# Layer 1 attention: the causal mask of the row maxima is added by VectorE's max instruction instead of by TensorE matmuls; one copy in layer 0 becomes a max

## The reference, cut to what matters

```
scores = jnp.einsum('bthd,bshd->bhts', q, k) / np.sqrt(HD)
causal = jnp.tril(jnp.ones((seq, seq), dtype=bool))
scores = jnp.where(causal[None, None], scores, -jnp.inf)
attn = jax.nn.softmax(scores, axis=-1)
out = jnp.einsum('bhts,bshd->bthd', attn, v)
```

## Time and profile before

| | us |
|---|---|
| median of 3 runs | 1455.15 |
| lowest, highest | 1451.16, 1457.0 |
| the profiled execution | 1449.74 |
| its span, first to last instruction | 1448.0 |
| PE busy | 1243.9 (86%) |
| DVE busy | 979.8 (68%) |
| ACT busy | 690.4 (48%) |
| POOL busy | 381.1 (26%) |
| mean granted TensorE clock | 0.909 |

### The profile page before, as it was taken

The page is one execution under the profiler, slowest core; times in us unless marked ns, Lnnn a source line. Parts: engine busy times, 40 slices in busy tenths (PEclk is TensorE's granted clock), DMA queues, the critical chain, the costliest instruction groups (busy, mean ns, idle before and its releaser), DMA issues. The chain is left out here.

```text
span 1448.0 us, 20297 instructions
## 1 busy us (share of the span) xinstructions
PE 1243.9 (86%) x7132; PEld 753.8 (52%) x7132; DVE 979.8 (68%) x1750; ACT 690.4 (48%) x1319; POOL 381.1 (26%) x243
## 2 busy tenths in 40 slices
PE   4779999999999999579999967358988888789997
PEld 3444454545455454348888845323433333347886
DVE  4747656565655642579999956757777664448998
ACT  2242544444353434336666644314666657326664
POOL 0036465746656568000000000302111111020000
PEclk9899999999999999689999968657999988869998
DMA  3101202011120200046766500051222201021321
GB/s 109 42 16 36 51 19 66 16 50 34 36 45 16 46 15 31 0 102 138 158 152 142 128 1 1 6 120 37 51 64 63 50 21 39 26 64 44 112 73 30
DMA packets 51471, 81.54 MB, mean 56 GB/s; under 512 B 16748, under 2 KB 34452, under 8 KB 47444
## 3 DMA queue, kind: packets, MB, share of 16 engines
q1 hardware_dynamic: 51100, 79.66, 22.6%
q10 hardware_dynamic: 288, 0.79, 0.5%
HBM read 63.75 MB, written 5.68 MB: 48 GB/s over the span
## 5 line engine op out<-in xcount | busy, mean ns | idle before, releaser
L1371 PE MATMUL ps<-qA 128*128 128x512 f32 x960 | 252.1, 399 | 14.6 <-POOL qA L1481 10.8
L641 DVE TENSOR_REDUCE mraw<-ps 128x1 f32<-128x512 f32 (+3 forms) x304 | 183.1, 654 | 71.2 <-PE ps L521 40.8
L744 ACT ACTIVATE shared<-ps 128x512 f32<-128x512 f32 (+1 forms) x216 | 118.8, 565 | 209.0 <-PE ps L554 203.0
L1371 PEld LDWEIGHTS ps<-qA 128*128 128x128 f32 x960 | 181.1, 192 | 64.1 <-POOL qA L1481 12.5
L1143 ACT ACTIVATE shared<-ps 128x512 f32<-128x512 f32 (+2 forms) x320 | 154.5, 561 | 114.8 <-PE ps L1012 114.4
L1088 DVE TENSOR_REDUCE mraw<-ps 128x2 f32<-128x1024 f32 (+3 forms) x160 | 173.0, 1113 | 53.0 <-PE ps L996 36.7
L553 PE MATMUL ps<-qA,kH 128*128 128x512 f32 (+3 forms) x384 | 162.6, 433 | 4.1 <-DMA qB<-mT 2.4
L782 POOL TENSOR_TENSOR VP<-VP,shared 128x2048 f32<-128x2048 f32 (+3 forms) x40 | 129.6, 3240 | 62.8 <-ACT shared L744 60.6
L1435 ACT CAST qA<-shared 128x512 fp32r<-128x512 f32 x160 | 99.3, 621 | 93.1 <-DVE shared L1573 91.6
L1383 PE MATMUL ps<-qA,kH 128*128 128x512 f32 x480 | 136.6, 393 | 4.1 <-DVE qA L1497 4.0
L515 PE MATMUL ps<-kH,qA 128*128 128x512 f32 (+3 forms) x384 | 120.8, 380 | 17.3 <-DVE qA L631 9.3
(11 more groups left out here) (250 smaller groups left out, 1897.4 us busy)
## 6 DMA issues: line engine op xcount, KB each, us to landing
shared<-comb SPq DMA_DIRECT2D x92, 256.0 KB, 4.3
qB<-qA SPq DMA_DIRECT2D x16, 512.0 KB, 4.8
rB<-a0rec_dram SPq DMA_DIRECT2D x60, 128.0 KB, 2.8
shared<-comb SPq DMA_DIRECT2D x7, 1024.0 KB, 4.4
rB<-a1rec_dram SPq DMA_DIRECT2D x28, 128.0 KB, 2.7
e0wUp<-in_w SPq DMA_DIRECT2D x48, 64.0 KB, 4.6
qA<-q_split SPq DMA_DIRECT2D x24, 128.0 KB
q_split<-qA SPq DMA_DIRECT2D x4, 512.0 KB
```

The source lines that it names most:

```text
L641: nc.vector.tensor_reduce(out[:, h0:h0 + n_h, qt % 4], src, AX, ALU.max).then_inc(w_free, 1)
L744: nc.scalar.activation(probs(n)[:, hs[0]:hs[-1] + 1, lo:512], src, ACT.Exp, scale=scale)\
L1371: ins = nc.tensor.matmul(bank[0:M, :], w[par][:, at:at + M], h[:, cols], start=(r == 0), stop=(r == 2))
```

## The change

In layer 1 the four mask matmuls of a diagonal job are gone. DVE handles each head of such a job alone: one `tensor_tensor_reduce` adds a mask row block from the new tile `k.late` (zeros, and the 128 x 128 mask at its end), writes the sum back over the scores in PSUM, and reduces by max into `k.mraw`. Its operands are one tensor from PSUM and one from SBUF. Jobs off the diagonal keep their `tensor_reduce`. In layer 0 the fold for qc 0 becomes a max of the maxima with themselves. `halves` is neither loaded nor converted; `late` is built in `stage_load` ahead of the instruction that PE waits for. `wmod` and the experts' `wD` move into tiles that exist anyway (`k.oU`, `k.S64`).

```diff
-                pe.wait_ge(chain, 2)
+                pe.wait_ge(chain, 3)
...
                 link(nc.vector.tensor_copy(k.masks[:, :, :], masks[:, :, :]))
+                nc.vector.memset(k.late[:, 0:512 - P], 0.0)
+                link(nc.vector.tensor_copy(k.late[:, 512 - P:512], masks[:, 1, :]))
                 link(nc.vector.tensor_tensor(cT[:, :, :], cT[:, :, :], sig[:, :, :], ALU.mult))
...
-                link(nc.vector.tensor_copy(k.halves[:, :, :, :].rearrange("p a b n -> p (a b) n"), halves[:, :, :]))
...
                     if qc == 0:
-                        nc.vector.tensor_copy(k.mmax[:, 0:16], k.mraw[:, 0, 0:16]).then_inc(folded, 1)
+                        nc.vector.tensor_tensor(k.mmax[:, 0:16], k.mraw[:, 0, 0:16], k.mraw[:, 0, 0:16],
+                                                ALU.max).then_inc(folded, 1)
...
-                                                   start=(slot == 0), stop=not diagonal,
+                                                   start=(slot == 0), stop=True,
                                                    skip_group_check=True)
-                    if diagonal:
-                        n_j = len(js)
-                        for part in range(2):
-                            for i in range(2):
-                                rows = row_tile(i, 64)
-                                ends = pair[:, i, 0:n_j * w].rearrange("p (j w) -> p j w", w=w)[:, :, w - P:w]
-                                ins = nc.tensor.matmul(ends, k.halves[rows, 0, part, :],
-                                                       k.halves[rows, 1, part:part + 1, :].broadcast_to((64, n_j, P)),
-                                                       start=False, stop=(part == 1), skip_group_check=True)
                     ins.then_inc(x_full, 1)
...
-                    src = pair[:, :, 0:len(js) * w].rearrange("p i (j w) -> p i j w", w=w)
-                    nc.vector.tensor_reduce(out[:, :, js[0]:js[-1] + 1, qt % 4], src, AX, ALU.max).then_inc(x_free, 1)
+                    if ch * 512 + w == (qt + 1) * P:
+                        for slot, jj in enumerate(js):
+                            for i in range(2):
+                                ins = nc.vector.tensor_tensor_reduce(
+                                    pair[:, i, slot * w:(slot + 1) * w], pair[:, i, slot * w:(slot + 1) * w],
+                                    k.late[:, 512 - w:512], 1.0, MASKED, ALU.add, ALU.max, out[:, i, jj, qt % 4:qt % 4 + 1])
+                        ins.then_inc(x_free, 1)
+                    else:
+                        src = pair[:, :, 0:len(js) * w].rearrange("p i (j w) -> p i j w", w=w)
+                        nc.vector.tensor_reduce(out[:, :, js[0]:js[-1] + 1, qt % 4], src, AX, ALU.max)\
+                            .then_inc(x_free, 1)
```

More of the change, by code:

```diff
@@ L70, in stage_load @@
         sig = sb("cT_sig", [P, 2, B])
-        wmod = sb("wmod", [P, 2, 6 * D])
+        wmod = k.oU[:, 0:2, 0:6 * D]
         masks = k.rB[:, 4 * P:6 * P].rearrange("p (a n) -> p a n", a=2)
-        halves = k.rB[:, 0:4 * P].rearrange("p (a n) -> p a n", a=4)
         tmp = sb("mod_tmp", [P, 3, 8])
         first = [
-            (halves[:, :, :], a["halves"]), (cT[:, :, :], a["cT"]), (wmod[:, 0, :], a["wmod"][:, 0, :]), (k.ident[:, :], a["ident"]),
+            (cT[:, :, :], a["cT"]), (wmod[:, 0, :], a["wmod"][:, 0, :]), (k.ident[:, :], a["ident"]),
             (masks[:, :, :], a["masks"]), (wmod[:, 1, :], a["wmod"][:, 1, :]),
@@ L980, in max_job @@
                     w = keys_in(qt, ch)
-                    diagonal = ch * 512 + w == (qt + 1) * P
                     for slot, jj in enumerate(js):
@@ L1277, in stage_experts @@
         wUp = sb("wUp", [P, 2, 2 * MT * M])
-        wD = sb("wD", [P, 2, MT * D])
+        wD = k.S64[:, 0:2 * MT * D].rearrange("p (s n) -> p s n", s=2)
         bi = sb("bias", [P, 2, 2 * MT])
@@ L2112, in program @@
         k.masks = sb("masks", [P, 2, P], BF16)
-        k.halves = sb("halves", [P, 2, 2, P], BF16)
+        k.late = sb("late", [P, 512])
         k.mod = sb("mod", [P, 2, 6, B])
@@ L2233, in constants @@
     pos = np.arange(S, dtype=f)
[L2234 to L2238, removed]
     dec = np.exp(-pos / f(S)).astype(f).reshape(TPB, P).T
@@ L2255, in constants @@
         "sel64": sel64,
-        "ident": np.eye(P, dtype=f), "masks": masks, "halves": halves.reshape(P, 4, P), "dec": dec, "rope": rope,
+        "ident": np.eye(P, dtype=f), "masks": masks, "dec": dec, "rope": rope,
         "sel": sel, "sel8": sel8,
```

## The result

The changed kernel took 1472.7 us (median of 5 executions, 1454.56 to 1474.01) beside 1451.47 us for the kernel before (5 executions, 1446.7 to 1457.0). The ratio is 1.0122, with a 95% interval of 1.0089 to 1.0156. Measured again for the experiments, it was 1462.15 us (8 executions, 1454.26 to 1471.51) and a ratio of 1.0079 [1.0047, 1.0112]. So the change costs 0.8 to 1.2%, 11 to 21 us by the medians, where 7 us were forecast. The mean of all 13 executions is 1464.9 us, that of the 61 executions of the kernel before 1450.5 us: +14.4 us. The profiled execution of after took 1454.56 us and is the fastest of its five; the other four had a mean granted clock of 0.880 to 0.885, it had 0.901. That is the first hint of where the time goes.

What follows compares the result with a forecast made beforehand. DVE was taken to bound layer 1's first stretch and PE to lead the second; -0.4 + 0 + 5 + 2 = +6.6 us on the profiled 1449.74 made 1456.3, forecast as a median of 1462 us, range 1447 to 1488.

Steps and rivals of the forecast that it cites:

- The case that I gave 0.45: Whole kernel: the forecast's own case, 1453 to 1468 us, around a median of 1462; chance 0.45.
- DVE's price: Layer 1's diagonal jobs: a set of six costs DVE 8.0 us instead of 5.7, 2.3 us more.
- the half rate: Rival, layer 1's passes: writing back into PSUM makes a column cost twice, 1537 us; chance 0.05.
- The read that lets DVE's need pass 215 us: Rival, second stretch: accumulator reads drain DVE, decisive from about 0.13 us a read; 1487 us at 0.23; chance 0.20.
- The first stretch: Layer 1's attention, 954 to 992 us: DVE bounds, three sets add 6.9 us, less waits, +5 us.
- The second stretch: Layer 1's attention, 1000 to 1215 us: both engines nearly full, PE waits for DVE instead, +2 us.
- the first rival: Layer 1's attention: PE's masks were the bound, second stretch -8 us, whole change -5 us, 1450; chance 0.20.
- The clock: Rival, PE: more stalls bring more stretches at 1.2 GHz, a few us on any case; no chance of its own.
- The fold: Layer 0: the new max waits for POOL's addition as the copy did, 0 us, ends 0 and -7.
- the load stage: Start of the kernel: one DMA fewer, but a longer chain ahead of PE's first matmul, -0.4 us.

Runs made afterwards that it cites:

- e2_no_mask: The changed kernel with every job of layer 1 one plain reduction, its maxima taken over unmasked scores: 1454.97 us, ratio 1.0031 to the kernel before.
- e1_both: The changed kernel with the mask matmuls of before put back, so the mask is added twice: 1462.24 us, ratio 1.0096 to the kernel before.
- e3_fold: The kernel before with only layer 0's fold changed, a max of the maxima with themselves instead of a copy: 1450.7 us, ratio 1.0001.
- e5_gather: The kernel before with the gather of the softmax sums issued ahead of a later group's loads on SP's queue: 1480.5 us, ratio 1.0213.

## Why the prediction was right, and where it was not

The forecast of 1462 us and +0.5% had the right sign and lies 3 us from the mean of after's 13 executions, 1464.9, and 11 us below the median of the first five. But that is in good part luck: two terms were too high and one that was hardly counted made nearly the whole difference. Part of the nearness comes from the start, too: 1462 stands on a median of three, 1455.15, that lies 4.6 us above the mean of 61 executions. As a difference, 6.6 us were forecast and 14.4 measured. The case that I gave 0.45 (1453 to 1468) holds the mean and the second median, 1462.15, but not the first, 1472.7, which only the wide range of 1447 to 1488 takes in.

**DVE's price, term too high.** The sum took 8.0 us a set, with the read of the accumulator at 0.10 us and bounds of 0.06 and 0.23. Measured: 7.2 us, so pass and read together cost 0.05 us beyond the 0.60 us of a plain instruction of 512 columns, just below the lower bound of 0.06. ACT's read the earlier trace rows was the wrong neighbour: there the next instruction starts 0.09 us after the read, here in the same moment. Nothing of the half rate was seen: a pass that writes back over its source in PSUM (0.65 us) takes nearly the time of one that doesn't (0.60). The Trainium skill ("VectorE: DVE Perf Modes", Rules for kernel authors) asks to keep the number of instructions small; the sign held here, its price was 1.5 us for 26 more rows in a set. (The read that lets DVE's need pass 215 us comes out at 0.14 us by the prediction's own terms, not 0.13.)

**The first stretch, +5, too high.** In the kernel before, the first job's reduction starts at 955.56 and the fold of the second turn at 981.15, 25.6 us. After, it is 952.84 to 979.63, 26.8 us: +1.2, and to the fold behind the third set 35.9 instead of 34.3, +1.6, below the lower end of 3. A row was misread here. Of the wait of 9.1 us for the first job only 1.6 us lie in the window (954 to 955.56); it began at 946.5. So the other 7.4 us of idle time come later, DVE was busy for 80% and not full, and the bound that the term rests on was too hard: up to the third fold DVE is busy for 3.4 us more and idle for 1.8 us less. From the group's first score to the next group's first score (timeline of PE) it is 54.17 us instead of 50.75, +3.4, and this again holds a lower clock: 0.52 instead of 0.61 from 954 to 1010. It doesn't need DVE's passes: in e2_no_mask, where DVE has the work of before, it is 54.41 us.

**The second stretch, +2.** That both engines would be full was wrong: DVE is busy for 163 us, not above 180, and PE's waits for maxima and folds are 45.1 us, where they were 47.1, not several times more. With 1.5 us a set the working would have read 154 + 20 + 22.5 = 196 us for DVE, PE leads, and the stretch gets about 8 us shorter. That is the first rival, and at equal clock the runs bear it out: PE gets back 6.3 and 8.7 us (before to e2_no_mask, e1_both to after), at the lower edge of the 8 to 15 that I had counted for the stage or below it. The work of the whole change adds up to -1 us, where the sum had +6.6 and that rival -5.

**The clock, the step that failed.** It stood among the rivals with "a few us" that would come on top of any case, and in no term of the sum. By the table it was worth 15 us, the whole lengthening. The rows were there: 0.96 in the stretch, the falls of PE's clock behind its waits. What I missed is that the matmuls that I was taking away could be part of what held it. Between 950 and 1260 us PE ran at its lower level for 75 us before, 119 and 153 us in the two profiles of after, 129 without any mask, 94 with both, 61 with the mask twice. It shows well in the same 30 us of both profiles, before first (from 1190 to 1220), then after, which is 3 us further back in its work at the start of them and 11 us behind them:

```profile
1190.00:1220.00 30.00, 26.31 (x213) 11.00 (x213) 18.38 (x21) 19.95 (x42) 4.97 (x9) 1.00 0.10 25
```

```profile
1190.00:1220.00 30.00, 27.64 (x148) 11.22 (x151) 19.90 (x55) 15.86 (x33) 3.17 (x5) 0.63 0.10 24
```

PE is as busy in both and does 213 matmuls in the one and 148 in the other. Ahead of this low piece, which lasts from 1184.8 to 1212.1, PE stood still for the fold of a turn:

```profile
1180.81 0.46 PE L985 MATMUL ps<-kL,qA 64*128 64x512 f32 x2
1183.61 0.27 PE L975 MATMUL ps<-ident,mmax 128*16 128x128 f32 x1 [2.34 <-DVE mmax L1066]
```

The last jobs of a chunk leave PE earlier by their masks, and DVE is done with them later, which would make this gap grow, and it has: the longest wait of PE for a fold of this kind from 1000 to 1215 us is 2.3 us, where it was 1.7; with the masks off PE alone it is 2.0 (e2_no_mask), with the passes on DVE alone 2.1 (e1_both). The Trainium skill ("TensorE: Matmul & The Clock Gate", A second HAM failure mode: psum-queue depth-cycling) describes short idle times of PE between groups of matmuls, from cycling through PSUM, that make the clock go to and fro; the trace agrees so far that PE's gaps in this stage are 3.1 us at most and the clock goes up and down, with falls at 1127.8, 1158.5 and 1223.3 before and five after (the first at 1065.3, the last at 1184.8). Six of these eight falls come in a gap of 1.5 to 3.1 us or within 2.1 us behind it. But the length of a gap doesn't tell whether the clock falls. A row of PE's timeline with its gap and a window behind it, first for after, then for before:

```profile
1148.67 0.27 PE L975 MATMUL ps<-ident,mmax 128*16 128x128 f32 x1 [1.63 <-DVE mmax L1066]
...
1151.00:1164.00 13.00, 12.81 (x65) 5.76 (x66) 8.48 (x32) 6.54 (x15) 2.54 (x4) 0.50 0.34 85
```

```profile
1190.81 0.27 PE L974 MATMUL ps<-ident,mmax 128*16 128x128 f32 x1 [1.63 <-DVE mmax L1072]
...
1191.00:1215.00 24.00, 21.62 (x176) 9.10 (x175) 17.75 (x19) 16.00 (x33) 2.54 (x4) 1.00 0.12 30
```

The same gap of 1.63 us for a fold is followed by 13.6 us at the lower level in after, and by none for 32 us in before.

**What stays open** is why these matmuls hold the clock up and others don't. For the second stretch two explanations fall. It is not PE's busy share alone: with fillers PE was 94% busy at 0.80, without it 86% at 0.85. It is not the total of its gaps either: in the same 215 us PE is idle for 28.5 us before, 30.1 and 25.0 in the two profiles of after, 27.2 without mask and 13.5 with filler. That the masks stand right at the end of the jobs, where PE goes on to wait for DVE, is a guess that is left; no run here puts filler into just that place. In the first stretch the busy share is not ruled out. In the 38 us from the stage's first matmul PE is busy for 29.1 us before, and its clock first rises 36.9 us after that matmul; with the mask twice it is 30.9 and 36.5 us, in after 24.2 and 55.2, in e2_no_mask 25.3 and 62.2. (e1_both, with 28.4 and 56.9, fits this less well.) A fifth to a quarter of what after spends longer at the lower level arises here.

**The fold and the load stage** came as forecast. The fold is worth 0 (e3_fold, and 1.63 us in its row). In the load stage PE's chain ends as it did: the copy of the modulation's result starts at 18.27 us, where it was 18.29 before, so 0.0 instead of -0.4 us.

## What to carry to other kernels

Where a stage's TensorE clock is near full and the engine waits often and briefly, work taken off TensorE is not saved time until the granted clock has been looked at: here 6 us of matmuls fewer went with a clock that cost 10 us, and the same matmuls doubled cost nothing. Compare kernels by several executions with the clock beside each, since one profile can lie 10 us from the mean. And before moving arithmetic between engines, look at what stands in a DMA queue ahead of small transfers for which a busy engine waits: moving two of them ahead of twelve loads gave 16 us, but moving only the first lost 31.

## What the runs showed of the hardware

DVE's add and max in one pass, in place in PSUM with a mask from SBUF, costs 0.25, 0.38, 0.51 and 0.65 us from start to start for 128, 256, 384 and 512 columns of fp32; the read of its accumulator, a row of 142 ns, is in these figures, which are 0.05 us above those of a plain instruction. The issue of one load of a key tile on SP's queue took 0.65 to 0.73 us, and the twelve loads of a group 7.7 us for whatever stood behind them (e5_gather). A max of 16 columns with both inputs in SBUF lasted 1.63 us and ended with POOL's addition (e3_fold and after). And one kernel's time varies by 8.2 us for 0.01 of mean granted clock, with a correlation of -0.92 to -0.95 over its executions, which is most of the scatter seen here.
